# The slot tables of two expert routings: columns and rows dealt out over GpSimd, VectorE and ScalarE in turn, selections written by token first

## The reference

```python
x = layernorm(x + L0_attn(x))       # rmsnorm, 16-head linear attention, then the first expert layer
x = layernorm(x + L0_ffn(x))        # layernorm, router, then the second expert layer
# either expert layer, 4096 tokens, 8 experts, top 2:
probs = softmax(xf @ router_W + router_b)
topk_probs, topk_idx = top_k(probs, 2)
for eid in range(8):
    idx = first CAPACITY (1280) token-choice pairs, in order of token, with topk_idx == eid
    h = mlp(xf[tok])                 # gelu (first layer) or silu(g) * u (second layer)
    out = out.at[tok].add(gate[:, None] * h)
```

## Time and profile before

| | before |
|---|---|
| median of 3 runs | 1633.08 us (1632.31 to 1634.97) |
| profiled execution, its own time | 1631.68 us |
| span of the profiled execution | 1629.9 us |
| busy: TensorE matmul | 1520.2 us (93%) |
| busy: VectorE | 1046.6 us (64%) |
| busy: ScalarE | 736.8 us (45%) |
| busy: GpSimd | 786.6 us (48%) |
| mean granted TensorE clock | 0.956 |

### The profile page before, as it was taken

How to read it: one execution, slowest core, us unless ns; L and a number is a source line. 1 busy time by engine, 2 the same in 40 slices (tenths; PEclk the granted TensorE clock), 3 DMA queues, 4 the chain that set the end, 5 groups by cost and what they waited for, 6 DMA issues and landing times. The chain is left out here.

```text
span 1629.9 us, 37588 instructions
## 1 busy us (share of the span) xinstructions
PE 1520.2 (93%) x11761; PEld 1451.8 (89%) x11761; DVE 1046.6 (64%) x2953; ACT 736.8 (45%) x1698; POOL 786.6 (48%) x795
## 2 busy tenths in 40 slices
PE   6999996699999999999967999999999999999990
PEld 4777774699999999999866999999999999999990
DVE  5888886676766676676465655565565665565553
ACT  3555552454545455555344434434343434343324
POOL 3778884156656665665241334334334434434420
PEclk9999997599999999999985999999999999999995
DMA  7011010223433433342332132313213231411216
GB/s 245 33 35 35 32 36 33 93 44 93 98 62 78 99 92 50 91 126 42 89 138 94 33 104 33 107 29 86 56 26 107 36 103 27 113 30 27 34 19 212
DMA packets 63715, 119.07 MB, mean 73 GB/s; under 512 B 14384, under 2 KB 52784, under 8 KB 61488
## 3 DMA queue, kind: packets, MB, share of 16 engines
q0 software_dynamic: 35840, 42.38, 16.0%
q1 hardware_dynamic: 27824, 76.07, 12.8%
HBM read 79.71 MB, written 38.71 MB: 73 GB/s over the span
## 5 line engine op out<-in xcount | busy, mean ns | idle before, releaser
L855 POOL DMA_INDIRECT acc<-E_ysb,IDX x160 | 258.2, 1614 | 135.5 <-ACT E_ysb L945 66.3
L982 DVE TENSOR_TENSOR E_hraw<-E_sg,bank 128x256 f32<-128x256 f32 x320 | 134.6, 421 | 286.1 <-ACT E_sg L918 286.1
L850 POOL DMA_INDIRECT E_mg<-meta,IDX x160 | 150.9, 943 | 337.1 <-DVE E_gate L966 311.2
L1035 PE MATMUL bank<-E_xT,ws 128*128 128x256 f32 x960 | 272.4, 284 | 5.0 <-DVE E_xT L957 5.0
L1036 PE MATMUL bank<-E_xT,ws 128*128 128x256 f32 x960 | 271.9, 283 | 0.0
L1037 PE MATMUL bank<-E_xT,ws 128*128 128x256 f32 x960 | 271.7, 283 | 0.0
L993 DVE TENSOR_TENSOR E_hT<-E_hraw,E_hT 128x256 fp32r<-128x256 f32 x640 | 259.5, 416 | 0.0
L989 DVE CAST E_hT<-E_hraw 128x256 fp32r<-128x256 f32 x640 | 203.2, 318 | 58.5 <-ACT E_hraw L921 51.6
L918 ACT ACTIVATE E_sg<-bank 128x256 f32<-128x256 f32 x320 | 121.6, 384 | 256.4 <-PE bank L1037 254.6
L1035 PEld LDWEIGHTS bank<-E_xT,ws 128*128 128x128 f32 x960 | 183.2, 191 | 6.0 <-issue 5.8
L1035 PE MATMUL bank<-ws,E_hT 128*128 128x256 f32 x640 | 183.8, 287 | 0.0
(11 more groups left out here) (195 smaller groups left out, 4045.8 us busy)
## 6 DMA issues: line engine op xcount, KB each, us to landing
wraw<-in_w_ffn SPq DMA_DIRECT2D x8, 3072.0 KB, 10.5
wraw<-in_w_moe SPq DMA_DIRECT2D x8, 2048.0 KB, 8.0
X<-acc SPq DMA_DIRECT2D x16, 512.0 KB, 6.9
X<-in_x SPq DMA_DIRECT2D x8, 512.0 KB, 9.3
xn<-A_xn SPq DMA_DIRECT2D x32, 128.0 KB, 1.7
acc<-X SPq DMA_DIRECT2D x32, 128.0 KB, 1.7
acc<-X SPq DMA_DIRECT2D x8, 512.0 KB, 2.9
out<-C_xo SPq DMA_DIRECT2D x8, 512.0 KB, 2.8
```

Source lines behind the costliest of these rows:

```text
L850: nc.gpsimd.indirect_dma_start(out=mg[:, j, :], out_offset=None, in_=meta_dram, in_offset=at_slots(u, j)).then_inc(s_gm, 16)
L855: nc.gpsimd.indirect_dma_start(out=acc_dram, out_offset=at_slots(u, j), in_=ysb[:, j, :], in_offset=None, compute_op=ALU.add).then_inc(s_y ...
L982: V.tensor_tensor(hraw[:, f % RING, :], sg[:, f % RING, :], bank[f % RING][:, UW:2 * UW], ALU.mult).then_inc(s_hm, 1)
L1035: nc.tensor.matmul(out, wh, mh, start=first, stop=False)
```

## The change

The split of the tables goes by n instead of by a bound. GpSimd makes the 32 columns with odd n, VectorE the 32 with even n. VectorE makes the 21 rows with n % 3 == 2, ScalarE the other 43. VectorE still goes through n in order and makes for each n its column, its row, both or none. TensorE waits for GpSimd's columns on a semaphore of its own. The tile `sel` is laid out by token first, so that VectorE writes it in the order in which it reads, and TensorE's two counting matmuls read it with a step of 8 elements; their results stay as they were. GpSimd's columns stand behind the constants and the clearing of semaphores in the first routing, and behind the normalisation of X in `between_phase`.

```diff
-DVE_PAIRS = 14
-ACT_PAIRS = 2 * NT - DVE_PAIRS
+PAIRS = [(n, n // 2, n % 2) for n in range(2 * NT)]
+POOL_COLS = [n for n in range(2 * NT) if n % 2 == 1]
+DVE_COLS = [n for n in range(2 * NT) if n % 2 == 0]
+DVE_ROWS = [n for n in range(2 * NT) if n % 3 == 2]
+ACT_ROWS = [n for n in range(2 * NT) if n % 3 != 2]
...
-        self.sel = sb("sel", [P, E, NT], BF16)
+        self.sel = sb("sel", [P, NT, E], BF16)
...
-        for n in range(ACT_PAIRS):
-            T, c = n // 2, n % 2
+        for n, T, c in PAIRS:
+            if n in DVE_ROWS:
+                continue
             nc.scalar.activation(self.row[:, n, :], self.iota, ACT.Sign, bias=self.brow[:, c, T:T + 1]).then_inc(self.s_row, 1)
+
+    def token(self, n, T):
+
+        return self.tok2[:, T:T + 1] if n in DVE_ROWS else self.cst[:, C_TOK + T:C_TOK + T + 1]
+
+    def columns(self, pool):
+        nc = self.nc
+        pool.wait_ge(self.s_set, 3)
+        pool.wait_ge(self.s_pc, 2)
+        for n, T, c in PAIRS:
+            if n in POOL_COLS:
+                nc.gpsimd.tensor_scalar(self.col[:, n, :], self.iota[:, 0:SC], self.pcf[:, 1, c, T:T + 1], self.token(n, T),
+                                        ALU.is_equal, ALU.mult).then_inc(self.s_colp, 1)
...
-        V.tensor_tensor(self.sel[:, :, :].rearrange("p e t -> p t e"), oh[:, 0, :, :], oh[:, 1, :, :], ALU.add).then_inc(self.s_sel, 1)
+        V.tensor_tensor(self.sel[:, :, :], oh[:, 0, :, :], oh[:, 1, :, :], ALU.add).then_inc(self.s_sel, 1)
...
-        for n in range(2 * NT):
-            T, c = n // 2, n % 2
-            by_act = n < ACT_PAIRS
-            token = cst[:, C_TOK + T:C_TOK + T + 1] if by_act else self.tok2[:, T:T + 1]
-            V.tensor_scalar(self.col[:, n, :], self.iota[:, 0:SC], self.pcf[:, 1, c, T:T + 1], token, ALU.is_equal,
-                            ALU.mult).then_inc(self.s_col, 1)
-            if not by_act:
+        for n, T, c in PAIRS:
+            if n in DVE_COLS:
+                V.tensor_scalar(self.col[:, n, :], self.iota[:, 0:SC], self.pcf[:, 1, c, T:T + 1], self.token(n, T), ALU.is_equal,
+                                ALU.mult).then_inc(self.s_col, 1)
+            if n in DVE_ROWS:
                 V.tensor_scalar(self.row[:, n, :], self.iota, self.pcf[:, 0, c, T:T + 1], 0.5, ALU.is_ge,
                                 ALU.subtract).then_inc(self.s_rowd, 1)
...
-        cols = self.sel[:, :, :].rearrange("p e t -> p (e t)")
+        cols = self.sel[:, :, :].rearrange("p t e -> p e t")
...
-        for n in range(2 * NT):
-            pe.wait_ge(self.s_col, n + 1)
-            if n < ACT_PAIRS:
-                pe.wait_ge(self.s_row, n + 1)
+        for n, T, c in PAIRS:
+            if n in POOL_COLS:
+                pe.wait_ge(self.s_colp, POOL_COLS.index(n) + 1)
             else:
-                pe.wait_ge(self.s_rowd, n - ACT_PAIRS + 1)
+                pe.wait_ge(self.s_col, DVE_COLS.index(n) + 1)
+            if n in DVE_ROWS:
+                pe.wait_ge(self.s_rowd, DVE_ROWS.index(n) + 1)
+            else:
+                pe.wait_ge(self.s_row, ACT_ROWS.index(n) + 1)
...
             nc.clear_and_free_semaphores(used)
+            R.columns(pool)
...
                     nc.gpsimd.tensor_scalar(X[:, n, :], X[:, n, :], rs[:, n:n + 1], nb[:, n:n + 1], ALU.mult, ALU.add).then_inc(s_x2, 1)
+            R.columns(pool)
```

More of the change, by code:

```diff
@@ L607, in __init__ @@
         self.s_v, self.s_ex, self.s_dl, self.s_sel, self.s_rank = map(sem, ("v", "ex", "dl", "sel", "rank"))
-        self.s_set, self.s_pc, self.s_row, self.s_rowd, self.s_col = map(sem, ("set", "pc", "row", "rowd", "col"))
+        self.s_set, self.s_pc, self.s_row, self.s_rowd, self.s_col, self.s_colp = map(sem, ("set", "pc", "row", "rowd", "col", "colp"))
         self.s_f, self.s_fs, self.s_idx, self.s_meta, self.s_ms = map(sem, ("f", "fs", "idx", "meta", "ms"))
```

## The result

| | before | after |
|---|---|---|
| median of 8 runs | 1633.01 us | 1639.53 us (1638.2 to 1640.59) |
| ratio, 95% interval | | 1.0037 (1.0026 to 1.0048) |
| span of the profiled execution | 1629.9 us | 1637.7 us |
| GpSimd busy | 786.6 us | 828.5 us |
| first table to last matmul, routing 1 / 2 | 17.84 / 17.84 us | 21.66 / 21.68 us |

The ratio is worth 6.0 us, 4.2 to 7.8 by its interval; the medians differ by 6.5. The forecast was 1632.0 within 1622.5 to 1639.5. The time lies outside it on the slow side, by 0.03 us: what has to be explained is the 7.5 us from the forecast, not the edge.

The account below looks back on a forecast made before the run. The table loop in each routing was taken as the bound: ScalarE's rows 14.6 us, TensorE's pace the last 3. Per routing +0.33 - 0.85 = -0.52 us, twice -1.0, from 1633.08 to 1632.0; range 1622.5 to 1639.5.

Parts of the forecast that it names:

- What bounds the loop: Loop of 64 tables in each routing: ScalarE's rows set 14.6 us, TensorE's own pace the last 3.
- the sum's frame: Both fenced routings shift the program's end equally: +0.33 - 0.85 = -0.52 us each, -1.0 for two.
- the rise that the prediction left open: TensorE's clock rising above half in the new loops: 0.9 us sooner each, 1.8 in all; forecast took no rise.
- ScalarE's 12.6 us: Table loop: ScalarE's 43 rows at 0.293 us each.
- VectorE's 11.5 without hindrance: Table loop: VectorE's 32 columns at 0.232 us plus 21 rows at 0.20, if engines did not hinder each other.
- The selections: Before the table loop: add falls from 1.27 to 0.42 us, stepped read free; gain 0.85 us, range 0.06 to 0.85.
- GpSimd's price p: Time per GpSimd column in the table loop, built from mult and add: 0.387 us, bounds 0.34 and 0.55.
- Lockstep: Table loop: one VectorE table per GpSimd column; last matmul at 18.18 us, 0.33 later than before; chance 0.45.
- the rule of the Trainium skill: GpSimd and VectorE exclude each other for whole instructions in the table loop: +11 us per routing, 1654; chance 0.05.
- C: Rival: lockstep with a dearer GpSimd column, routing break-even at p = 0.403, 1642.4 us at 0.55; chance 0.17.
- B: Rival: VectorE keeps its pace beside GpSimd in the table loop; -4.65 us per routing, 1623.8; chance 0.33.
- The chances: Whole program, with about 0.2% (3.3 us) as what can be told: faster 0.33, same 0.45, slower 0.22.

Follow-up runs that it names:

- beside: Kernel before, plus idle GpSimd mult and add beside the table loops (30 on 80 elements, 20 on 256); last matmuls at 17.96 and 19.61 us.
- forms2: Kernel before, plus 40 GpSimd tensor_scalar instructions of eight forms in the last phase; on 80 elements, mult and add 0.39 us, is_equal and mult 0.62.
- psum_src: Changed kernel with VectorE's tables reading their counting row from PSUM instead of SBUF; 1637.29 us, ratio 1.003 (1.0018 to 1.0041).

## Why the prediction was wrong, point by point

**What bounds the loop; the sum's frame.** Right. The routings moved by the loop's and the selections' differences, twice. The granted clock was 0.50 in every loop, also in the last 9.7 us of the first loop after, in which TensorE was busy for 9.62, so the rise that the prediction left open did not come. ScalarE's 12.6 us came as computed, and VectorE's 11.5 without hindrance were 12.3 with it, 0.5 us of it by being held up.

**The selections.** The add is 0.42 us as forecast, but the stepped read costs 0.48 us, within the bounds 0 to 0.79, of which I took 0. The reason given, that at the low clock TensorE has time for it, was wrong: 256 stepped columns take longer even so. Term: -0.85 forecast, -0.37 measured, 1 us too much over the two routings.

**GpSimd's price p, the step that failed.** I put it at 0.387 from mult and add. For mult and add it is 0.39; for the comparison it is 0.615 alone, 0.72 on average beside VectorE and 0.672 over the loop. "Both nearest forms fit one price" was true and said nothing on a third operation. The earlier trace rows held a warning: the power took 0.55 us on one element where mult and add took 0.21 on 32, so GpSimd's price can hang on the operation. I used it as a bound, and as an upper one it was still too low, since that row has one element and the comparison costs 3.4 ns for each. The Trainium skill (GPSIMD Engine Reference, section Elementwise — side-by-side cycle accounting) gives 1.03 cycles per element for bodies of up to two operations, by my estimate 0.86 ns at the 1.2 GHz by which its own example counts. The 0.86 ns of mult and add in the earlier trace rows agree with that, the comparison's 3.4 ns do not.

**Lockstep, the second step that failed.** The exclusion is there: GpSimd goes from 0.615 to between 0.66 and 0.79 beside VectorE and back when VectorE's source is in PSUM. Its size was wrong. I took all of the 0.43 us that GpSimd still needed after getting free in the earlier trace rows, less the elements' share, as time in which it holds VectorE out. The run `beside` shows that most of it is not: beside 80 elements VectorE lost nothing, beside 256 it lost 0.08 us on every second column. And where they meet on small tiles GpSimd gives way more than VectorE: in the changed kernel's loop it lost 1.7 us over 17 columns, VectorE 0.5 over 53 tables.

This also answers the rule of the Trainium skill (SBUF — State Buffer, section Who interferes with whom) that the prediction set against rows. That the two contend, the traces show; a blocking for the whole instruction they do not: in `beside` one GpSimd instruction and two VectorE columns take 0.467 us together, where 0.39 + 2 x 0.23 = 0.85 would be due if none ran beside another.

**The rivals.** What came is C's cause, a dearer column with break-even far below its price, in B's company: VectorE keeps pace, as B had it. The prediction had tied C to lockstep. By the prediction's own sum, lockstep with the comparison's own p = 0.615 gives 18.18 + 32 x (0.615 - 0.387) = 25.5 us to the last matmul. What was measured, 21.66, is the count times the measured pace: 0.15 + 31 x 0.672 + 0.63 = 21.61 for the end of the last column, and TensorE right behind. The two errors went against each other, +7.3 us a loop for the price and -3.8 for the lockstep that was not there, so the total missed the edge of the range by only 0.03 us. That is luck and no credit to the sum.

**The chances.** 0.22 for slower was too low. The forecast took for known a price that no row showed, and its upper bound belonged to an operation chosen for being slow, not to a measured comparison.

## What to carry to other kernels

Price an instruction on GpSimd by its operation as well as by its size: a form measured for mult and add says nothing about a comparison, and a test of a few instructions in a quiet phase is cheap beside a wrong split. When work is dealt out by turns over several engines into one ordered consumer, the end is count times price of the dearest share; solve for the shares that make these equal (here 16 to 21 columns, not 32) instead of halving. When two engines exclude each other on a shared path, look at who loses time on tiles of the real size: here VectorE lost nothing beside 80 elements and 0.08 us on every second column beside 256, where the prediction had held its tables to GpSimd's pace.

## What the runs showed of the hardware

A GpSimd tensor_scalar with is_equal and mult costs 3.4 ns an element (0.48 us on 40, 0.62 on 80, 0.78 on 128) against 0.86 for mult and add, and at 80 elements it costs the same whether it writes fp32 or fp32r; two pointers in place of immediates add 0.05 us to it at 80 elements (`forms2`).

GpSimd's comparison takes 0.05 to 0.18 us longer from start to start beside VectorE's tensor_scalar instructions with a source in SBUF (changed kernel), and no longer than alone when their source is in PSUM, 0.617 us (`psum_src`). The Trainium skill (SBUF — State Buffer, section Who interferes with whom) states that a VectorE instruction with at most one input in SBUF and outside the 2-port modes does not contend with GpSimd, and the 0.617 agrees with that.

TensorE reads 256 bf16 columns with a step of 8 elements in about 0.43 us start to start (286.51 to 286.94) at the low clock, where the second matmul on the same columns in order started 0.16 us behind the first.
